# A two-layer cross-attention on one core: the product with Wv in two halves of 256 columns in place of one pass of 512

## The reference, cut to what matters

```python
def layer(emb, latent, Wq, bq, Wk, bk, Wv, bv, gamma, beta):
    q = jnp.einsum('bte,ef->btf', emb, Wq) + bq
    k = jnp.einsum('bml,le->bme', latent, Wk) + bk
    v = jnp.einsum('bml,le->bme', latent, Wv) + bv
    w = jnp.einsum('bte,bme->btm', q, k) * scale
    w = jax.nn.softmax(w, axis=1)
    pred = jnp.einsum('btm,bme->bte', w, v)
    x = pred + emb
    mu = jnp.mean(x, axis=-1, keepdims=True)
    var = jnp.var(x, axis=-1, keepdims=True)
    return (x - mu) * jax.lax.rsqrt(var + EPS) * gamma + beta
x = layer(x, ctx_512, *L0_weights)
x = layer(x, ctx_512, *L1_weights)
```

## Time and profile before

| | |
|---|---|
| median of 3 runs | 1041.25 us (1040.89 to 1045.34) |
| the profiled execution: its time | 1043.51 us |
| its span, first to last instruction | 1041.6 us |
| mean granted clock of TensorE, share of 2.4 GHz | 0.983 |
| PE busy | 999.5 us, 96% |
| PEld busy | 937.7 us, 90% |
| DVE busy | 873.1 us, 84% |
| ACT busy | 667.3 us, 64% |
| POOL busy | 564.4 us, 54% |
| the chain of work that ended last, share on PE | 89% |

### The profile page before, as it was taken

How to read it: one execution, slowest core, us unless ns; L and a number is a source line. 1 busy time by engine, 2 the same in 40 slices (tenths; PEclk the granted TensorE clock), 3 DMA queues, 4 the chain that set the end, 5 groups by cost and what they waited for, 6 DMA issues and landing times.

```text
span 1041.6 us, 23850 instructions
## 1 busy us (share of the span) xinstructions
PE 999.5 (96%) x6928; PEld 937.7 (90%) x6928; DVE 873.1 (84%) x2607; ACT 667.3 (64%) x1873; POOL 564.4 (54%) x517
## 2 busy tenths in 40 slices
PE   5689999999999999999999999999999999999984
PEld 4579999999999999999999999999999999999973
DVE  3567889888988888889988888898898888888863
ACT  1336766766766677666766776666667667666643
POOL 0022556566555565665555656655565665555653
PEclk9889999999999999999999999999999999999997
DMA  9753444443454444444544443445444434453101
GB/s 176 168 127 62 96 96 103 98 98 79 99 106 96 108 96 97 95 82 98 111 97 101 99 100 84 89 101 112 94 98 101 97 81 97 105 113 78 48 18 36
DMA packets 384828, 100.07 MB, mean 96 GB/s; under 512 B 318352, under 2 KB 368400, under 8 KB 384784
## 3 DMA queue, kind: packets, MB, share of 16 engines
q1 hardware_dynamic: 381952, 98.21, 44.0%
q10 hardware_dynamic: 2832, 1.32, 0.8%
HBM read 84.81 MB, written 14.68 MB: 96 GB/s over the span
## 4 chain that ended last, share of the span: by engine, by line
PE 89%; SPq 3%; issue 2%; DVE 2%; POOL 2%; ACT 1%; DMA 1%; POOLq 0%; DVEq 0%; ACTq 0%
PE oq_bank L592 27%; PE score_bank L565 8%; PE score_bank L566 8%; PE score_bank L570 8%; PE pv_bank L623 6%; PE pv_bank L618 5%; PE pv_bank L619 5%; PE oq_bank L541 5%; PE oq_bank L536 5%; PE oq_bank L537 5%; PE t_bank L501 3%; PE oq_bank L598 2%; PE t_bank L518 1%; DMA x<-in_L_xattn_Wv_dram 1%; SPq L353 1%
## 5 line engine op out<-in xcount | busy, mean ns | idle before, releaser
L592 PE MATMUL oq_bank<-probs,raw 125*128 125x224 f32 x1536 | 316.6, 356 | 6.2 <-ACT probs L761 6.2
L592 PEld LDWEIGHTS oq_bank<-probs,raw 125*128 125x128 f32 x1536 | 284.5, 192 | 8.1 <-issue 4.3
L752 ACT ACTIVATE probs<-probs,neg_max 125x224 f32<-125x224 f32 x384 | 180.6, 472 | 148.8 <-DVE neg_max L987 148.7
L1172 POOL TENSOR_TENSOR psum<-probs 125x672 f32<-125x672 f32 x64 | 103.3, 1614 | 295.4 <-ACT probs L761 295.4
L565 PE MATMUL score_bank<-qT_hi,cT_hi 128*125 128x224 f32 x768 | 200.3, 287 | 4.4 <-ACT cT_hi L709 3.1
L566 PE MATMUL score_bank<-qT_hi,cT_lo 128*125 128x224 f32 x768 | 189.8, 274 | 0.0
L761 ACT ACTIVATE probs<-probs,rsum 125x224 f32<-125x224 f32 x384 | 153.2, 472 | 10.0 <-DVE rsum L995 8.8
L1215 POOL TENSOR_TENSOR y_out<-z,gamma_row 112x512 f32<-112x512 f32 x62 | 93.3, 1526 | 117.3 <-ACT z L785 117.3
L565 PEld LDWEIGHTS score_bank<-qT_hi,cT_hi 128*125 128x125 f32 x768 | 145.9, 190 | 9.4 <-ACT cT_hi L709 4.1
L570 PE MATMUL score_bank<-qT_lo,cT_hi 128*125 128x224 f32 x768 | 147.5, 274 | 0.0
L566 PEld LDWEIGHTS score_bank<-qT_hi,cT_lo 128*125 128x125 f32 x768 | 146.1, 190 | 0.0
(11 more groups left out here) (106 smaller groups left out, 2007.8 us busy)
## 6 DMA issues: line engine op xcount, KB each, us to landing
raw<-in_ctx_dram SPq DMA_DIRECT2D x64, 375.0 KB
cb<-in_ctx_dram SPq DMA_DIRECT2D x256, 92.0 KB
xb<-in_x_dram SPq DMA_DIRECT2D x128, 112.0 KB, 3.0
x<-in_x_dram SPq DMA_DIRECT2D x32, 448.0 KB, 3.5
out_dram<-y_out SPq DMA_DIRECT2D x31, 448.0 KB, 6.7
cb<-in_ctx_dram SPq DMA_DIRECT2D x128, 3.5 KB
y<-in_L_xattn_Wq_dram SPq DMA_DIRECT2D x2, 512.0 KB, 5.3
Wq_next<-in_L_xattn_Wq_dram SPq DMA_DIRECT2D x2, 512.0 KB, 5.6
```

The lines of the kernel that those rows point to most:

```text
L592: ins = nc.tensor.matmul(o, raw[0:MP, u.slot, c, cols], probs[0:MP, u.par4, c, :], start=(c == 0), stop=(c == MC - 1))
L752: ins = act.activation(probs[0:MP, u.par4, c, :], probs[0:MP, u.par4, c, :], ACT.Exp, bias=neg_max[0:MP, u.par4, c:c + 1], scale=-1.0, acc ...
```

## The change

Each `h` of `pv_product` runs over the 512 columns of Wv in two halves. All six matmuls are done for columns 0 to 255 first, then all six for columns 256 to 511, into the two halves of the same bank. The stationary operands, `oT_hi` and `oT_lo`, are the same in both halves, and each matmul loads its own. The waits stand in the first half of h = 0 alone, and `pv_ready` is raised by the last matmul of the second half.

```diff
-                o = pv_bank[h][0:TP, :]
                 rows = slice(h * TP, (h + 1) * TP)
-                for l in range(LC):
-                    if h == 0:
-                        pe.wait_ge(oT_hi_done, u.n(m=2, add=l - 1))
-                    nc.tensor.matmul(o, oT_hi[:, l, rows], Wv_hi[:, u.layer, l, :], start=(l == 0), stop=False)
-                    nc.tensor.matmul(o, oT_hi[:, l, rows], Wv_lo[:, u.layer, l, :], start=False, stop=False)
-                for l in range(LC):
-                    if h == 0:
-                        pe.wait_ge(oT_lo_done, u.n(m=2, add=l - 1))
-                    ins = nc.tensor.matmul(o, oT_lo[:, l, rows], Wv_hi[:, u.layer, l, :], start=False, stop=(l == LC - 1))
+                for half in range(2):
+                    of = slice(half * E // 2, (half + 1) * E // 2)
+                    o = pv_bank[h][0:TP, of]
+                    for l in range(LC):
+                        if h == 0 and half == 0:
+                            pe.wait_ge(oT_hi_done, u.n(m=2, add=l - 1))
+                        nc.tensor.matmul(o, oT_hi[:, l, rows], Wv_hi[:, u.layer, l, of], start=(l == 0), stop=False)
+                        nc.tensor.matmul(o, oT_hi[:, l, rows], Wv_lo[:, u.layer, l, of], start=False, stop=False)
+                    for l in range(LC):
+                        if h == 0 and half == 0:
+                            pe.wait_ge(oT_lo_done, u.n(m=2, add=l - 1))
+                        ins = nc.tensor.matmul(o, oT_lo[:, l, rows], Wv_hi[:, u.layer, l, of], start=False, stop=(l == LC - 1))
                 ins.then_inc(pv_ready, 1)
```

## The result

The changed kernel takes 1050.21 us, the median of 5 runs (1048.04 to 1054.09), against 1041.25 us for the kernel before (median of 5, 1040.47 to 1045.34). The ratio is 1.008 with a 95% interval of 1.0047 to 1.0113: 5 to 12 us slower. The profiled execution has a span of 1052.2 us, 10.6 us more than that of before, and is the slowest of its five runs.

What follows compares the result with a forecast made beforehand. The prediction took PE, busy without idle time from 200 to 900 us, as the bound. It added 5.4 us of matmul pace and 6.3 us of waits, 11.7 us, to 1041.25 for 1053 us, range 1046 to 1062.

Steps and rivals of the forecast that it cites:

- The first term: All 768 matmuls with Wv: two of 256 columns take 238 ns where one of 512 took 231, +5.4 us.
- the fourth rival: Matmuls with Wv: 256 columns stream at the bare clock, 109 ns, a pair 218, -10 us; chance 0.07.
- The second term: Group h = 0: PE needs `oT_lo` for l = 1 earlier and waits, net 0.45 us, 14 times, +6.3 us.
- In proportion: Matmuls with Wv: a pair of 256 costs what one of 512 did, only the waits' +6.3 us remain; chance 0.18.
- Fixed cost: Matmuls with Wv: each pays some 17 ns, so +12.0 us of pace plus 6.3 of waits, 1059.6 us; chance 0.17.
- No stall: Low-part wait in h = 0: POOL-DVE race reverses or other waits shrink as much; +5.4 us alone, 1046.7; chance 0.12.
- The other side: Matmuls with Wv at the bare clock, -10 us: 1031 us without the waits, 1037.5 with them; chance 0.07.

Runs made afterwards that it cites:

- only h = 1 split: Against the kernel before, only the group h = 1, which waits for no operand, is split in halves, h = 0 stays whole: 1044.67 us.
- POOL waiting in both kernels: Kernel before and changed kernel, each with POOL's layer 1 product with gamma waiting for both residuals of the next unit: 1039.32 and 1044.85 us.

## Why the prediction was right, point by point

**What bounds the kernel.** PE without idle time from 200 to 900 us meant that what PE needs more, the kernel needs more. In h = 1, where nothing waits, PE's added matmuls make a turn without the collision longer by 0.08 us (*only h = 1 split*), and nothing takes that back.

**The first term.** 119 ns was forecast for 256 columns, and 118 came; with that a pair costs 236 to 237 ns where one matmul took 231, 5 to 6 more. The turns say the same: 0.15 us over the 24 pairs of a turn without the collision is 6.3 ns each, 0.25 over the 48 of two turns, with POOL waiting in both kernels, 5.2. 768 pairs are then 4.0 to 4.8 us; the prediction had 7 ns and 5.4 us. What made it right was to take the one 224-column matmul whose weights were there early (105 ns) and not the run of them (110), which is the pace of their weight loads. The bound from that run, 123 ns and +12 us, would have been the fixed cost, and the proportion would have been 116. Nor did the 256s go at the bare 109 of the fourth rival. The rule of the Trainium skill for a matmul alone ("TensorE: Matmul & The Clock Gate", "Back-to-back issue gap") gives 109 ns for 256 columns and 216 for 512; the trace has 118 and 231 in this format, so the measurement decides against it for both, and its difference for a pair, +2.5 ns, is under the measured 5 to 6.

**The second term.** The delay of the group in a turn with the collision was forecast as 0.60 us and is 0.60. What comes back at the score product was put at 0.15, so that 0.45 would remain; the turns show 0.40, or 0.46 when the pace of that turn is taken from the kernels where POOL waits. The mechanism is thus right: the same stretched residual of 1.8 us, the same place, the same price. The count is right by luck. The forecast took all 14 waits of before as alike, though it had found a collision for 11 only. Of the three others one is gone and another is new, which makes 14 again. And single turns cost more than the regular 0.40 to 0.46: the one with the late transfer is 1.6 us longer than the regular ones with the collision, and the one with the new wait at 156.3 us grew from 29.79 to 30.55. The total of PEld's waits, 12.5 us against the 9 to 10 of the prediction, has the same reason: in the loop each wait grew by 0.35 us as said (0.27 to 0.62), and the two long ones bring the rest.

**The sum.** Over the 30 turns between the marks four profiles split the +10.9 us. With POOL waiting in both kernels the split costs +3.3 us (894.30 to 897.59), its pace. POOL's wait saves 2.8 us without the split and 10.4 with it, so the collisions, with what they set off, cost 7.6 us more. This rests on one execution of each kernel. The forecast of 11.7 was 5.4 + 6.3; measured like this, the pace was put too high by 1 to 2 us and the waits too low by about 1, and the errors partly cancel. The medians differ by 9.0 us (5 to 12), which can't tell these apart. The profiled spans differ by 10.6, but that is no further proof: the changed kernel's profile is the slowest of its five, it was 1.9 us ahead at the first mark and lost 1.6 behind the last.

**The rivals.** *In proportion* is excluded by h = 1 alone: its turn without the collision is 0.08 us longer, where this rival has none. *Fixed cost* would have made the turns 24 x 15.7 = 0.38 us longer. *No stall* didn't happen by itself, and the experiment that brings it about shows that its price, +5.4, was too high: +2.6 us by the medians and +0.5 between the marks, since without the collision the 0.24 us that it cost in each such turn before are gone as well. *The other side* failed at the pace.

## What to carry to other kernels

Cutting a matmul in two costs more than the added instructions: it also changes how far into a group each operand is needed, and a wait that was hidden under long matmuls ahead of it comes out as soon as that cover shrinks. Before such an edit, compare for each awaited operand the time at which it is ready with the time at which it would be needed, in every kind of turn that the trace shows, not in an average. And where one engine is always busy, look at the turns whose length differs: here one wait on POOL removed a collision with DVE and brought 3 us, about a third of what the split had cost.

## What the runs showed of the hardware that was not expected

A matmul in the `float32r` format has a straight-line pace once its weights are there: about 60 ns for 128 columns, 105 for 224 (this one worked out in the prediction), 118 for 256, 176 for 384 and 231 for 512, so 0.44 ns a column at a granted clock of 1.00 and a few ns beside. That is slower than a bare 2.4 GHz (0.417 ns) for each column; why, no run here tells.

A residual on DVE and a product on POOL do not run side by side here: the one that starts second is held up by most of what is left of the other. If POOL is ahead by 5 to 16 ns, DVE's residual lasts 1.82 us in place of 0.75; if DVE is ahead by 0.16 us, POOL's product lasts 1.75 in place of 1.29. In this kernel it is POOL that can wait without harm, and by programming that wait the time falls from 1042.24 to 1039.32 us.

Why the collision comes in every second turn of the loop and in none of the turns written out can be read from the trace. ACT's z starts 0.10 us before `oT_hi` is done in all of them. DVE's first residual starts 0.03 us after `oT_hi` is done in most turns, but 0.12 us after it in the 11 turns with the collision, and that is what lets POOL be first. In just these 11 turns DVE's sequencer carries out an arithmetic instruction of line 1015 right ahead of the first residual, 0.084 us before it starts. All the instructions of that line in the kernel before:

```profile
L1015 DVEq ALU_OP  x44: 40/40/40, 214.3 to 830.5; - x44
```

Line 1015 is the wait for `z_done` in `residual`, whose threshold depends on the loop's counter. It executes such an instruction only in the loop, four times a pass. One of the four runs while DVE stands idle ahead of a first residual; in the pass read closely the others run while DVE is busy. The changed kernel (line 1017 there) and the two kernels with POOL's wait have it in the same place, and in the latter two DVE starts just as late (0.12 us) without a collision. So the late start is there whether or not POOL is; it doesn't come from the collision. No run moved that instruction, so this cause is read off and not tested.
